# An attention and feed-forward kernel on one core: squared queries kept as two bf16 halves, and a new hand-written order of work on five engines

## What is computed

```
h = layernorm(x)
q = rmsnorm(h @ Wq) * gq ; k = rmsnorm(ctx @ Wk) * gk ; v = ctx @ Wv     (per head of 128)
x = x + tanh(g_xattn) * softmax(q k^T / sqrt(128)) v @ Wo
scale = mean|W| ; Wt = clip(round(W / scale), -1, 1) * scale              (three FFN matrices)
x = x + tanh(g_ffn) * bitlinear(silu(bitlinear(x, Wg)) * bitlinear(x, Wu), Wd)
```

## Time and profile before

| | |
|---|---|
| median of three runs | 2347.47 us |
| the profiled execution | 2351.92 us, span 2350.1 us |
| TensorE busy | 2215.9 us, 94% |
| VectorE busy | 1837.9 us, 78% |
| ScalarE busy | 1612.3 us, 69% |
| GpSimd busy | 1273.9 us, 54% |
| mean granted TensorE clock | 0.977 |

### The profile page before, as it was taken

The page is one execution under the profiler, slowest core; times in us unless marked ns, Lnnn a source line. Parts: engine busy times, 40 slices in busy tenths (PEclk is TensorE's granted clock), DMA queues, the critical chain, the costliest instruction groups (busy, mean ns, idle before and its releaser), DMA issues. The chain is left out here.

```text
span 2350.1 us, 45689 instructions
## 1 busy us (share of the span) xinstructions
PE 2215.9 (94%) x16187; PEld 1573.9 (67%) x16338; DVE 1837.9 (78%) x4171; ACT 1612.3 (69%) x3398; POOL 1273.9 (54%) x1623
## 2 busy tenths in 40 slices
PE   5889999999999999999999999999999999769999
PEld 3567777777776777777777777776767777534444
DVE  5788877787777787877777778777777777569997
ACT  4677777777776777666767777676767667546665
POOL 4555656565656555656666676767666655200000
PEclk9899999999999999999999999999999999989999
DMA  5776776666677776656676767676777665635665
GB/s 144 169 149 136 124 146 127 139 133 129 131 130 144 123 144 126 132 105 139 132 145 136 151 129 149 135 138 134 143 145 132 133 109 111 171 95 139 141 140 126
DMA packets 921748, 317.53 MB, mean 135 GB/s; under 512 B 864912, under 2 KB 882608, under 8 KB 921264
## 3 DMA queue, kind: packets, MB, share of 16 engines
q1 hardware_dynamic: 921520, 314.61, 66.6%
HBM read 82.09 MB, written 19.40 MB: 43 GB/s over the span
## 5 line engine op out<-in xcount | busy, mean ns | idle before, releaser
L1181 POOL TENSOR_TENSOR ksplit<-khat,ksplit 128x512 bf16<-128x512 f32 (+1 forms) x384 | 455.5, 1188 | 74.0 <-ACT ksplit L667 73.1
L893 DVE TENSOR_TENSOR khat<-keys_ps,krs 128x512 f32<-128x512 f32 (+1 forms) x384 | 263.4, 686 | 287.4 <-POOL krs L1175 287.2
L1175 POOL TENSOR_TENSOR krs<-kvar,minus_half 128x4 f32<-128x4 f32 (+1 forms) x384 | 387.1, 1008 | 32.0
L689 ACT ACTIVATE prob<-score_ps,nbias,qrs 100x361 f32<-100x361 f32 x512 | 328.6, 647 | 71.8 <-DVE nbias L911 70.4
L1172 POOL TENSOR_SCALAR kvar<-kss 128x4 f32<-128x4 f32 (+1 forms) x384 | 89.1, 232 | 531.9 <-DVE kss L883 530.0
L672 ACT ACTIVATE ksq<-keys_ps 128x512 f32<-128x512 f32 (+1 forms) x384 | 227.8, 596 | 188.5 <-PE keys_ps L25 188.4
L698 ACT ACTIVATE psplit<-prob,rden 100x361 bf16<-100x361 f32 x512 | 304.3, 595 | 64.9 <-DVE rden L917 64.2
L923 DVE SCALAR_TENSOR_TENSOR psplit<-prob,rden,psplit 100x361 bf16<-100x361 f32 x512 | 317.5, 629 | 4.2 <-ACT psplit L698 0.6
L901 DVE TENSOR_REDUCE nmax<-score_ps 100x1 f32<-100x361 f32 x512 | 268.3, 524 | 54.5 <-PE score_ps L25 54.3
L667 ACT ACTIVATE ksplit<-khat 128x512 bf16<-128x512 f32 (+1 forms) x384 | 240.5, 626 | 98.0 <-DVE khat L893 97.3
L24 PE MATMUL keys_ps<-wk_split,ctxT 128*128 128x512 bf16 (+1 forms) x768 | 293.8, 383 | 6.8
(11 more groups left out here) (132 smaller groups left out, 5323.1 us busy)
## 6 DMA issues: line engine op xcount, KB each, us to landing
stage<-in_ffn SPq DMA_DIRECT2D x96, 256.0 KB, 3.2
ctx_raw<-in_ctx SPq DMA_DIRECT2D x31, 256.0 KB, 3.5
xin<-in_x SPq DMA_DIRECT2D x32, 200.0 KB
res_rows<-in_x SPq DMA_DIRECT2D x32, 200.0 KB
x_rows<-res_rows SPq DMA_DIRECT2D x32, 200.0 KB
xin<-x_rows SPq DMA_DIRECT2D x25, 256.0 KB, 2.7
xres<-x_rows SPq DMA_DIRECT2D x25, 256.0 KB, 3.0
out<-xres SPq DMA_DIRECT2D x25, 256.0 KB, 2.0
```

Of the source, the lines that this page charges most:

```text
L689: act.activation(prob[:, h, :], score_ps[h % 2][0:SQ, 0:SK], ACT.Exp, bias=nbias[:, b, h:h + 1], scale=qrs[:, v // 2 % 2, r:r + 1], accum_ ...
L893: dve.tensor_tensor(khat[0:KV[t], k, :].rearrange("p (h d) -> p h d", h=G), keys_ps[k][0:KV[t], :].rearrange("p (h d) -> p h d", h=G), rs, ...
L1175: pool.tensor_tensor(krs[0:KV[t], k, :], kvar[0:KV[t], k, :], minus_half[0:KV[t], 0:G], ALU.pow).then_inc(krs_done, 1)
L1181: pool.tensor_tensor(ksplit[0:KV[t], t, 1, :], khat[0:KV[t], (u + t) % 2, :], ksplit[0:KV[t], t, 0, :], ALU.subtract).then_inc(k_lo_done, 1)
```

## The change

1. The squared queries are kept as two bf16 halves, qsq_hi and qsq_lo, in one buffer qsq_split with a zeroed tail. ScalarE squares each half of the queries twice: in float32 into qsq (now for 2 heads, one buffer) and in bf16 into qsq_hi. GpSimd subtracts (query_squares_lo). TensorE sums the halves with 16 bf16 matmuls of 128 columns of weights. yT, the transposed output, lies in qsq_split.
2. The squares' use of a shared bank comes after heads out and the second transpose of x.
3. The order in two_turns is new on all engines. TensorE and GpSimd stand in the diff. ScalarE, for a pair of turns: key squares 0, 1; queries high 0 and its high square; weight chunk; square 0; exp 0; keys_hi 0; queries high 1 and its high square; key square 2; square 1; next key square 0; probs_hi 0; exp 1; keys_hi 1; mixed_hi 0; keys_hi 2; mixed_hi 1; exp 2; probs_hi 1; next key square 1; exp 3; heads out 0, 1; probs_hi 2, 3; next key square 2; next keys_hi 0 and 1; exp 0 and 1 of the next scores; next keys_hi 2; weight chunk; probs_hi 0; exp 2, 3; mixed_hi 0, 1; probs_hi 1, 2, 3. VectorE: key sums 0, 1; row_max 0, row_bias 0, row_max 1; scale_keys 0; queries_lo 0; scale_keys 1; row_bias 1; row_sum 0; key sum 2; queries_lo 1; next key sum 0; row_max 2; scale_keys 2; row_bias 2; probs_lo 0; row_sum 1; mixed_lo 0, 1; row_max 3; row_sum 2; row_bias 3; next scale_keys 0; next key sum 1; probs_lo 1; row_sum 3; heads out 0, 1; probs_lo 2, 3; next key sum 2; next scale_keys 1; row_max and row_bias 0, 1 of the next scores; next scale_keys 2; row_max 2; row_sum 0, 1; row_bias 2; squares out (qvar); row_max 3, row_bias 3; mixed_lo 0; row_sum 2, 3; probs_lo 0 to 3; mixed_lo 1.
4. A weight chunk is loaded one turn ahead into one of two buffers (stage slots 0 and 3); w_out and w_abs move into stage slot 2, and the kernel's own stage slots go from 5 to 4, so that seven slots become six.
5. SP loads the next context after the transposes of a turn instead of ahead of them; split_ctx waits for a use that is an earlier one.

```diff
         for u in [] if first else range(1, UNITS, 2):
             v = u + 1
             if more_queries(u, last):
-                order += [("q", u, 0)]
-            if more_queries(u, last):
-                order += [("q", u, 1)]
+                order += [("q", u, 0), ("q", u, 1)]
             order += [("m", u, 0), ("m", u, 1)]
             if u == UNITS - 5 and not last:
                 order += [("x", 0)]
-            if more_queries(u, last):
-                order += [("qss", u)]
             order += [("o", v, 0), ("o", v, 1)]
             if u == UNITS - 5 and not last:
                 order += [("x", 1)]
+            if more_queries(u, last):
+                order += [("qss", u)]
             if has_mixed(v, last):
                 order += [("m", v, 0), ("m", v, 1)]
...
+    def query_use(i, u):
+        n = i * UNITS + u // 2 * 2 - 3
+        return use(n // UNITS, ("q", n % UNITS, QD - 1))[0]
...
-        qsq = sb("qsq", [P, G, QT], F32)
+        qsq, qsq_split = sb("qsq", [P, TWO, QT], F32), sb("qsq_split", [P, 2 * G * QT + PAD], BF16)
+        qsq_hi, qsq_lo = (qsq_split[:, a * G * QT:(a + 1) * G * QT].rearrange("p (h q) -> p h q", h=G)
+                          for a in range(2))
...
-        w_raw, w_out = stage[:, 0, :], sb("w_out", [P, CHUNK], BF16)
+        w_raw, w_out = [stage[:, 0, :], stage[:, 3, :]], stage[:, 2, 0:CHUNK // 2].bitcast(BF16)
+        w_abs = stage[:, 2, CHUNK // 2:CHUNK // 2 + MATRICES * CHUNKS].rearrange("p (m n) -> p m n", m=MATRICES)
...
+            sp.wait_ge(nat_ready, 2 * KVT)
+            load_ctx(1, 0, ctx_raw)
...
             def load_chunk(i, u):
+                i, u = (i, u + 1) if u < UNITS else (i + 1, 1)
                 n, m = sum_chunk_of(i, u), tern_chunk_of(i, u)
-                if n is not None and n > 0:
-                    sp.wait_ge(w_summed, n)
-                if m is not None:
-                    sp.wait_ge(w_summed, MATRICES * CHUNKS)
-                    if m > 0:
-                        sp.wait_ge(w_rounded, m)
                 if n is not None or m is not None:
+                    c = n if m is None else MATRICES * CHUNKS + m
+                    if m is not None:
+                        sp.wait_ge(w_summed, min(c - 1, MATRICES * CHUNKS))
+                        if m > 1:
+                            sp.wait_ge(w_rounded, m - 1)
+                    elif n > 1:
+                        sp.wait_ge(w_summed, n - 1)
                     rows, cols = chunk_at(n if m is None else m)
-                    sp.dma_start(w_raw[:, :], w_ffn[rows, cols]).then_inc(w_raw_in, 16)
+                    sp.dma_start(w_raw[c % 2], w_ffn[rows, cols]).then_inc(w_raw_in[c % 2], 16)
...
                     eng.wait_ge(kT_in[b], keys_turned(i, u))
+                    eng.wait_ge(shared_free, query_use(i, u) + 1)
...
             def query_squares(i, u):
                 ps = shared_bank(i, ("qss", u))
-                eng.wait_ge(q_sq_done, i * (NG * QD) + ((u + 3) // 2 + 1) * QD)
+                eng.wait_ge(q_sqlo_done, i * (NG * QD) + ((u + 3) // 2 + 1) * QD)
                 for b in range(2):
                     for h in range(G):
-                        last = pe.matmul(ps[0:SQ, b * G + h:b * G + h + 1], qsq[:, h, b * SQ:(b + 1) * SQ],
-                                         ones[:, 0:1], start=True, stop=True)
+                        out, hi, lo = ps[:, b * G + h:b * G + h + 1], h * QT + b * SQ, (G + h) * QT + b * SQ
+                        pe.matmul(out, qsq_split[:, hi:hi + P], ones[:, 0:1], start=True, stop=False)
+                        last = pe.matmul(out, qsq_split[:, lo:lo + P], ones[:, 0:1], start=False, stop=True)
                 last.then_inc(shared_done, 1)
...
                     queries(i, u, 0)
                 if su:
                     scores(i, u + 1, 0), scores(i, u + 1, 1)
+                if qu:
+                    queries(i, u, 1)
                 if ku:
                     keys(i, u + 2, 2)
-                if qu:
-                    queries(i, u, 1)
+                if kv:
+                    keys(i, v + 2, 0)
                 if su:
                     scores(i, u + 1, 2)
-                mixed(i, u, 0, par)
+                mixed(i, u, 0, par), mixed(i, u, 1, par)
                 if su:
                     scores(i, u + 1, 3)
-                if kv:
-                    keys(i, v + 2, 0)
-                mixed(i, u, 1, par)
                 if kv:
                     keys(i, v + 2, 1)
                 if new_x:
                     turn_x(i, 0)
-                if qu:
-                    query_squares(i, u)
-                if i == TERN_PAIR - 1 and u == 1:
-                    weight_totals(i)
                 heads_out(i, v, 0), heads_out(i, v, 1)
                 if new_x:
                     turn_x(i, 1)
                 if kv:
                     keys(i, v + 2, 2)
+                if qu:
+                    query_squares(i, u)
+                if i == TERN_PAIR - 1 and u == 1:
+                    weight_totals(i)
+                project(i, v, 0), project(i, v, 1)
                 if sv:
                     scores(i, v + 1, 0), scores(i, v + 1, 1)
-                project(i, v, 0), project(i, v, 1)
-                if sv:
-                    scores(i, v + 1, 2)
                 project(i, v, 2), project(i, v, 3)
                 if sv:
-                    scores(i, v + 1, 3)
+                    scores(i, v + 1, 2), scores(i, v + 1, 3)
...
             def queries_square(i, u, k):
                 n, p = use(i, ("q", u, k))
+                ps = shared_ps[p][:, 0:TWO * QT].rearrange("p (h q) -> p h q", h=TWO)
                 eng.wait_ge(shared_done, n + 1)
-                act.activation(qsq[:, k * TWO:(k + 1) * TWO, :],
-                               shared_ps[p][:, 0:TWO * QT].rearrange("p (h q) -> p h q", h=TWO),
-                               ACT.Square).then_inc(q_sq_done, 1)
+                if started(i * (NG * QD) + (u + 3) // 2 * QD + k):
+                    eng.wait_ge(q_sqlo_done, i * (NG * QD) + (u + 3) // 2 * QD + k)
+                act.activation(qsq[:, :, :], ps, ACT.Square).then_inc(q_sq_done, 1)
+            def queries_square_hi(i, u, k):
+                n, p = use(i, ("q", u, k))
+                ps, heads = shared_ps[p][:, 0:TWO * QT].rearrange("p (h q) -> p h q", h=TWO), slice(k * TWO, (k + 1) * TWO)
+                eng.wait_ge(shared_done, n + 1)
+                act.activation(qsq_hi[:, heads, :], ps, ACT.Square).then_inc(q_sqhi_done, 1)
...
                 if ku:
...
                 eng.wait_ge(q_hi_done, i * (NG * QD) + ((u + 3) // 2 * QD + k + 1))
+                eng.wait_ge(q_sq_done, i * (NG * QD) + ((u + 3) // 2 * QD + k + 1))
+                eng.wait_ge(q_sqhi_done, i * (NG * QD) + ((u + 3) // 2 * QD + k + 1))
...
+            def query_squares_lo(i, u, k):
+                heads = slice(k * TWO, (k + 1) * TWO)
+                n = i * (NG * QD) + ((u + 3) // 2 * QD + k + 1)
+                eng.wait_ge(q_sq_done, n)
+                eng.wait_ge(q_sqhi_done, n)
+                pool.tensor_tensor(qsq_lo[:, heads, :], qsq[:, :, :], qsq_hi[:, heads, :],
+                                   ALU.subtract).then_inc(q_sqlo_done, 1)
...
-                    if not (isinstance(j, int) and j == 0):
-                        eng.wait_ge(shared_done, use(j - 1, ("m", 1, CC - 1))[0] + 1)
+                    if j > 1:
+                        eng.wait_ge(shared_done, use(j - 2, ("m", UNITS - 1, CC - 1))[0] + 1)
...
             def two_turns(i, u):
                 v, last, par = u + 1, i == PAIRS - 1, i % 2
-                ku, kv, qu = has_keys(u, last), has_keys(v, last), more_queries(u, last)
+                ku, su, qu = has_keys(u, last), has_scores(u, last), more_queries(u, last)
+                kv, sv, mv = has_keys(v, last), has_scores(v, last), has_mixed(v, last)
                 new_ctx, b = u in (1, 3) and not last, u // 2
                 if ku:
                     key_scale(i, u + 2, 0)
                 if u == UNITS - 5 and not last:
                     deviation(i, 1)
                 if ku:
-                    key_scale(i, u + 2, 1), keys_lo(i, u + 2, 0)
-                    key_scale(i, u + 2, 2), keys_lo(i, u + 2, 1), keys_lo(i, u + 2, 2)
-                if new_ctx:
-                    split_ctx(i + 1, b, 0, 1 - par, ctx_raw)
+                    key_scale(i, u + 2, 1)
+                round_chunk(i, u)
+                if qu:
+                    query_squares_lo(i, u, 0)
+                if ku:
+                    keys_lo(i, u + 2, 0), key_scale(i, u + 2, 2)
                 if kv:
                     key_scale(i, v + 2, 0)
+                if ku:
+                    keys_lo(i, u + 2, 1), keys_lo(i, u + 2, 2)
                 if qu:
-                    query_scale(i, u)
-                round_chunk(i, u)
+                    query_squares_lo(i, u, 1)
                 if kv:
-                    key_scale(i, v + 2, 1), keys_lo(i, v + 2, 0)
```

(23 more changed lines are left out.)

180 lines of the change are left out of this document (90 added, 90 removed).

## The result

The changed kernel is slower: 2428.16 us median (2421.95 to 2433.37, 4 runs) against 2345.8 (2342.74 to 2347.76, 4 runs) beside it, a ratio of 1.0351 (95% interval 1.0322 to 1.038). The forecast was 2276 us.

A forecast was written before the change was run, and what follows sets the result against it. TensorE, busy 94% of the span, was taken as the bound. Squares 40 + 4, clock 18, waits 14 and prologue -1 make 75 us gained; with 3.5 us added for ternary pairs the forecast was 2276 us, range 2243 to 2325.

The forecast's parts named there:

- What bounds the kernel: Whole kernel: TensorE, busy 94% of the span, is the bound; 5.4 us a pair of sequences are lost, 75 in all.
- Part 1: Squares on TensorE: 16 bf16 matmuls at 40 ns instead of 85, gaining 0.72 us a pass, 40 + 4 us.
- Part 2: Squares' extra work on ScalarE and GpSimd: busy 23.1 and 21.5 (ternary 22.8) of some 29.5 us; prologue +1 us.
- Part 3: New order, one pair of turns walked on all engines: no forced wait, 28 us of waits against 42, gain 14.
- The margins at khat: Spare time of scale_keys before TensorE wants the keys: 0.5 and 0.65 us, 0.4 in turns with new context.
- the consumers come over 10 us later: SP: context's load moved behind the transposes and a chunk's load a turn earlier, with over 10 us before their use.
- the chain through xT: New-x turn: first heads_out wants the bank chain through xT, oT_lo and the second transpose, about 0.8 us a pair.
- The clock: New-x turn: TensorE's granted clock should hold once the waits around the squares are gone, gaining 18 us.
- D: Rival: the clock still falls once a pair, the squares being a stretch with hardly a column; 2294 us, chance 0.10.
- The sum: Squares 40 + 4, clock 18, waits 14, prologue -1: 75 us gained; with 3.5 us for ternary pairs, 2276 us.
- C: Rival, slower: late scale_keys 1 makes TensorE wait for keys; 2372 us at 1.6 us a pair of turns, chance 0.10.
- B: Rival: new waits fill thin margins at keys behind scale_keys 1, 0.5 us in 60 pairs of turns; 2306 us, chance 0.25.

## Why the prediction was wrong

**What bounds the kernel.** Right: TensorE. But "so its own work and its losses are what a change can move" led past VectorE, whose durations were taken as constants.

**Part 1, the squares.** The mechanism was right and the term too small: 25 ns a matmul, 61 us instead of 44, beyond the lower bound of 30 ns. The granted clock was full there.

**Part 2, the squares elsewhere.** "Neither becomes the bound by its sum" is true and missed the price. GpSimd's two subtractions a pair of turns were costed as GpSimd's time alone, but each stops a row_bias that meets it. Alone in the old order the whole part cost 42 us, and with the one-input row_bias in both kernels it cost nothing (2328.19 against 2327.54 us).

**Part 3, the walk.** This is the step that failed: it allowed 28 us of waits on TensorE in the middle, and 132 were recorded. It walked each engine at the mean durations of before, and never looked at row_bias, whose durations in the trace of before would have shown that something held it (shortest, median, longest in ns):

```profile
L911 DVE TENSOR_TENSOR nbias<-nmax,qrs x512: 143/160/1118, 47.8 to 2037.6; 100x1 f32<-100x1 f32 x171
```

On the walk's own terms much came true: VectorE's idle time for krs fell from the 251 us of the earlier trace rows to 16 in the middle, the waits for qvar went, and khat's was 7.1 us. The margins at khat held; what broke the walk was a term that it had at a fixed size, and two chains that it left out or sized too small (below).

The Trainium skill ("SBUF — State Buffer", Who interferes with whom) says that a VectorE instruction with two SBUF inputs contends with a GpSimd instruction that reads SBUF, that whichever issues first holds what they share for the whole instruction while the other is fully blocked, and that one SBUF input, outside of what it calls the 2-port modes, does not contend. The traces agree for subtractions on GpSimd: 561 ns with two inputs, 209 with one, 155 with one of the two in PSUM, and ends that fall together with GpSimd's. They differ from it for krs, which GpSimd computes from SBUF too: in the kernel before, all 163 row_bias that start inside a krs last under 0.2 us. It was the rule that spoke against this change, and the prediction didn't weigh it.

**A second victim.** probs_lo reads prob and psplit from SBUF, and its mean is 665 ns after against 629 before (705 with the squares alone). The trace shows the same blocking there (engines by name, start and duration in us):

```profile
905.21 2.27 POOL L1199 TENSOR_TENSOR ksplit<-khat,ksplit 128x512 bf16<-128x512 f32 x2
906.31 1.57 DVE L938 SCALAR_TENSOR_TENSOR psplit<-prob,rden,psplit 100x361 bf16<-100x361 f32 x1
907.44 1.23 POOL L1208 TENSOR_TENSOR qsq_split<-qsq,qsq_split 128x400 bf16<-128x400 f32 x1
```

probs_lo has a median of 593 ns. In the changed kernel 121 of the 512 last over 0.7 us, and each of the 121 ends 0.38 to 0.40 us after the end of a GpSimd instruction; of the 391 others, 25 do. Before, it was 69, all of them so. The excess over 590 ns is 39 us after and 20 before; 94 of the 121 follow a split_ctx instruction. It works the other way too: the low half of the squares that starts at 907.44, while probs_lo is at work, takes 1.23 us instead of its median of 0.94. What this costs in time is open, as no kernel here gave probs_lo other inputs.

**The transposes.** "SP: ... the consumers come over 10 us later" was argued for the loads. For ctxT it was not asked. The change moved the first key tile of the new context forward on TensorE, and left its transposes on SP behind pT's and a chunk's load (SP's timeline after; the matmul from TensorE's):

```profile
928.91 3.15 SPq L326 DMA_TRANSPOSE pT<-psplit  x2
932.11 0.89 SPq L388 DMA_DIRECT2D stage<-in_ffn  x1
933.10 3.81 SPq L302 DMA_TRANSPOSE ctxT<-nat  x3
```

```profile
938.13 0.39 PE L23 MATMUL keys_ps<-wk_split,ctxT 128*128 128x512 bf16 x1 [2.25 <-DMA ctxT<-nat]
```

They are issued from 933.10 on and TensorE wants the first at 935.7. Its removal gave 55 us, the clock included: the second largest loss.

**The new-x turn.** Forecast at 0.8 us a pair for the chain through xT, it is 2.3 (32.2 us in 14):

```profile
908.47 0.56 PE L520 MATMUL shared_ps<-ident,xin 100*128 100x100 f32 x4 [0.69 <-DVE uT L892]
912.30 0.27 PE L23 MATMUL shared_ps<-uT,wv_hi 128*128 128x200 bf16 x1 [2.06 <-DVE xT_lo L892]
```

The transposes end at 909.03. xT_hi on ScalarE stands behind an exponential until 910.21, and xT_lo on VectorE behind khat, a layer norm, a key sum and probs_lo until 911.68. The reordering was worth 10 us; 24.3 us of the wait stay, and what would take them away was not tried.

**The clock.** 18 us were to come back; instead it cost 32.3 us in the middle against 23.9, by the same sum over stretches. The stand before the squares went, but two longer ones came in each pair, and the clock fell behind about half of them (0.61 and 0.54 from 912 us on, 0.51 and 0.64 from 1066 on). Of the forecast's rivals D saw a fall once a pair; its reason, the squares' pass itself, is not what happened.

**The sum.** In the fourteen pairs 68.5 us were to be gained and 66 were lost, a gap of 135. Measured against the forecast's terms: squares 14 better, clock 26 worse, recorded waits 100 worse (132 against the 28 and the 3.5 for ternary pairs). I go by waits, since the 48 us of idle time in the earlier trace rows hold some 6 us at keys' matmuls without a record (13131 records against 13248 after). Each wait hides another 0.165 us in the recorded length of its predecessor (0.25 us for a 200-column matmul that the next may follow after 0.0856); there are 123 waits instead of 62, which is 10 us more. That makes some 123. The other 12 us stay open. Outside of the pairs the first copy came 5.2 us later than in the earlier trace rows, where with the squares' gain some 3 less were forecast; GpSimd's low halves are waited for there, 3.5 us:

```profile
L547 PE MATMUL shared_ps<-ones,qsq_split 128*128 128x1 bf16 x512 | 33.4, 164 | 5.0 <-POOL qsq_split L1208 3.5 <-DVE oT_lo L892 1.4
```

By cause, from the experiments: 77 us blocked row_bias, 55.5 ctxT, 10 the order of xT, 142.5 in all. Cured together they give 140, to 2287.84, 12 us above the forecast. So the gain that the forecast counted exists; the change spent it, and more, at three places.

**The rivals.** C had the sign with a chance of 0.10, but not the mechanism: it wanted TensorE to wait for khat behind a late scale_keys, and that wait was 7.1 us. B, lateness spread over all turns, was likewise asked of khat.

## What to carry to other kernels

Before GpSimd work is added or bunched, list VectorE's instructions that read two tensors from SBUF, and look at the spread of their durations, not at their waits: a tiny one that is sometimes long is being held. Give it a pointer or PSUM in place of the second input (here one line, 21 us in the old kernel and 77 in the new). When a consumer is moved forward on one engine, move along each queue that feeds it: the walk must hold every producer's issue time, also those that the diff does not touch.

## What the runs showed of the hardware that was not expected

- A VectorE instruction over 100x1 elements with both inputs in SBUF took up to 2700 ns beside GpSimd's subtractions, and never over 160 with one of its inputs in PSUM. The stand is recorded as its duration, not as a wait.
- Two GpSimd subtractions back to back can hold it through both: 1.74 us from 951.82, while one subtraction takes 1178 ns on average. Of the row_bias that start in the first of two in the changed kernel, 49 end with the second and 38 with the first; what decides it is not shown.
- While GpSimd computes krs from four columns there was no such stand in the kernel before (at 868.44 us row_bias took 0.16 us inside a krs of 1.01) or after (111 inside a krs, all under 0.2 us). But with GpSimd's order changed back, 41 row_bias that start inside a krs end only with the key subtraction behind it, one of them 0.66 us ahead of that subtraction; why is open.
- A bf16 load of 128 columns with a one-column matmul goes at 25 ns start to start. The Trainium skill ("TensorE: Matmul & The Clock Gate", Weight-path perf modes) gives the fast load fourfold in theory, for fp8, and about twofold as measured. The 25 ns measured here, in bf16, are a quarter of the 99 ns that such a load is recorded to last in the queries. Whether the load or the matmul sets the 25 ns no run shows.
- 2.31 us without a matmul were followed by the lower clock at 1066 us, and 2.25 us at 938 were not: the stretch behind them ran at 1.00. The length of the stand alone doesn't tell: of the changed kernel's 14 waits for ctxT in the middle, 9 were followed by a lower clock (0.50 to 0.72 over the next 3 us) and 5 by the full one, the one of 3.72 us at 556 among these.
